# LSTM over image rows between two group norms: the convolved inputs kept as f32 and copied into the state banks by ScalarE

## The chip, the cores and the metric

The kernel runs on one core of a Trainium2 chip. The metric is the device time of one execution in microseconds (us). Three runs of the kernel before gave a median of 709.94 us, from 704.29 to 713.18 us.

## The reference

The input `x` is (32, 128, 32, 32) in f32: 32 images, 128 channels, 32 by 32 pixels. Two blocks follow, each `x = x + f(group_norm(x))` with 32 groups. `f` of the first block is a masked input convolution followed by an LSTM that steps over the 32 rows of the images; the state is 128 channels for 32 x 32 (image, column) positions:

```python
def step(carry, x_row):
    h, c = carry
    hc = conv(h, w_s2s) + b_s2s            # 1 x 3 over positions
    gates = (x_row + hc) @ w_ih.T + bias   # 4 x 128
    i, f, g, o = jnp.split(gates, 4, axis=-1)
    c = jax.nn.sigmoid(f) * c + jax.nn.sigmoid(i) * jnp.tanh(g)
    h = jax.nn.sigmoid(o) * jnp.tanh(c)
    return ((h, c), h)
```

`x_row` is the input convolution (1 x 3, its right tap masked to zero) of the normed images, one image row at a time. `f` of the second block is a 3 x 3 convolution whose weights are partly masked to their centre.

## The kernel before

Everything stays in on-chip memory, in `img` (128 channels x 32 images x 1024 pixels, four bytes a pixel). There are three stages, one after the other.

**Stage 1, the input convolution, one image at a time.** SyncE issues the loads (`load_x`), VectorE takes the statistics (`image_stats`) and the group norm's chain of small steps (`chain_mean`, `chain_var`, `chain_rstd`) for four images at once, seven images ahead of the convolution (`STATS_AHEAD`). ScalarE norms an image into `xn0` (`norm_image`). GpSimd or ScalarE, in turn, makes its f16 high part `hi0`, and GpSimd the rest `lo0`. TensorE's `input_conv` does twelve matmuls into two PSUM banks (`y_bank`). There are two slots of `xn0`, `hi0`, `lo0` and of pairs of banks. The result goes back to `img` as two f16 halves: ScalarE writes the high half (`high_xs`), VectorE the low one (`low_xs`). The weights are scaled, turned and split in between, at fixed places of each engine's program (`scale_weights` before image 7 is stored, `split_weights`, `last_weights`).

**Stage 2, the LSTM, in 96 items.** An item is one image row of one block of images: three blocks (`BLOCKS`) of 11, 10 and 11 images, so 352 or 320 columns. Every engine works through its own list of items in order, and semaphores tie them. TensorE's item `it` is:

- `close_conv(it)`: three matmuls, the right tap of the state convolution, which end the sum in the bank `zbank(it)` (there are two, used in turn);
- a wait for `z_lo_done`, and then `open_conv(it + 1)`: two matmuls with `spread` (a scaled identity) that bring the two f16 halves of the convolved input into the next bank, and six of the state convolution;
- a wait for `z_hi_done`, and twelve matmuls of the four gates of item `it`, the last two of the first pair after `z_lo`.

ScalarE's item `it` is the four gates of `it`, `high_z(it + 1)` (which reads `zbank(it + 1)` and writes `z_hi`), and `tc`, the tanh of the cell of `it`. VectorE forms the cell (L605, L609), `z_lo` of the next item (L590), the state and its two f16 halves (L614 to L619) and a transpose (L624). GpSimd multiplies the forget gate with the cell (L731) and adds the transposed state and the input into `img` (L739).

**Stage 3, the 3 x 3 convolution.** The change leaves it as it is but for the number that its chunks of statistics begin with.

Of the kernel before, what the change touches and what calls it, by code (L numbers as in the profile page):

```python
# [15 lines left out]
P = 128  # L16
# [12 lines left out]
XS_SCALE = 2.0 ** -14  # L29
# [10 lines left out]
CH = 4  # L40
CHUNKS = B // CH
GN_STEPS = 11
# [4 lines left out]
STATS_AHEAD = 7  # L47
# [24 lines left out]
def build_network(nc, x, w_i2s, b_i2s, w_s2s, b_s2s, w_ih, b_ih, b_hh, w_conv, b_conv, consts, out):  # L72
# [4 lines left out]
    with ExitStack() as ctx:  # L77
# [20 lines left out]
        bn = sb("bn", [P, CH, 2, 6], F32)  # L98
# [16 lines left out]
        with ExitStack() as s01:  # L115
# [13 lines left out]
            spread = sb("spread", [P, P], F16, s01)  # L129
            raw_cb = sb("raw_cb", [P, P], F32, s01)  # L130
            mask = sb("mask", [P, P], F32, s01)
            with ExitStack() as s0:
                xn0 = [sb(f"xn0{i}", [P, HW], F32, s0) for i in range(2)]
                hi0 = [sb(f"hi0{i}", [P, HW], F16, s0) for i in range(2)]
                lo0 = [sb(f"lo0{i}", [P, HW], F16, s0) for i in range(2)]
                raw_i = sb("raw_i", [P, P, 3], F32, s0)
                raw_s = sb("raw_s", [P, P, 3], F32, s0)
                raw_g = sb("raw_g", [P, GATES, P], F32, s0)
                raw_c = sb("raw_c", [P, P, 9], F32, s0)
                turn_i = sb("turn_i", [P, 2, P], F32, s0)  # L140
                turn_c = sb("turn_c", [P, 9, P], F32, s0)
            with ExitStack() as s1:
# [8 lines left out]
                hh = [sb(f"hh{i}", [P, B * W + 2], F16, s1) for i in range(2)]  # L151
                hl = [sb(f"hl{i}", [P, B * W + 2], F16, s1) for i in range(2)]
# [17 lines left out]
        spread_done = sem("spread_done")  # L170
# [23 lines left out]
        xs_hi_done = sem("xs_hi_done")  # L194
        xs_lo_done = sem("xs_lo_done")
# [40 lines left out]

        def padded(t, half, dh, dw):
# [20 lines left out]
        def xs_part(b, s, part):  # L258
            return img[:, b, H // 2 * s:H // 2 * (s + 1), part, :]
# [8 lines left out]

        def wgroup(n):
            return ps[:, 4 + n, 0:[2, 3, 4][n] * P].rearrange("p (a b) -> p a b", b=P)  # L270

        bias_T = ps[:, 4, 3 * P:4 * P]
        bias_ps = bias_T[96:97].rearrange("p (q n) -> p q n", q=Q)
        gate_bias_ps = ps[:, 5, 3 * P:3 * P + GATES]
# [3 lines left out]

        wconv_ps = ps[:, 4:7, 0:3 * P].rearrange("p d (e o) -> p d e o", o=P)
# [12 lines left out]
        def _(sp):  # L292
            def images(q, b, n):
                return img32[32 * q:32 * q + 32, b:b + n].rearrange("p b h w -> p b (h w)")

            def load_x(b):

                if b >= 2 * CH:

                    sp.wait_ge(x_in[b % (2 * CH)], QUARTERS_IN * (b // (2 * CH)))  # L300
                for q in QUARTERS:
                    sp.dma_start(images(q, b, 1), x_q[q, :, b:b + 1, :]).then_inc(x_in[b % (2 * CH)], 16)

            for b in range(STATS_AHEAD):
                load_x(b)
                if b == 0:
                    sp.dma_start(group_mean[:], consts[1]).then_inc(group_in, 16)
# [10 lines left out]
            for b in range(STATS_AHEAD, B):  # L318
                load_x(b)

            def place_blocks():

                sp.wait_ge(split_done, 4)
# [62 lines left out]
        def _(v):  # L386
# [23 lines left out]
            def bn_aggr(g):  # L410

                v.wait_ge(bn_done, 2 * CH * (g + 1))
                apart()
                for j in range(CH):
# [5 lines left out]
            def chain_mean(g):  # L420

                v.wait_ge(mean_ready, g + 1)
                v.tensor_tensor(dev[:], mv[:, :, 0], gn_ps[:, 0:CH], ALU.subtract).then_inc(gn_step, 1)
                v.tensor_tensor(dev_ps, mv[:, :, 0], gn_ps[:, 0:CH], ALU.subtract).then_inc(gn_step, 1)
                gn_wait(g, 2)
                v.tensor_tensor(dev2_ps, dev_ps, dev[:], ALU.mult).then_inc(gn_step, 1)
                gn_wait(g, 3)
                v.tensor_tensor(vdev[:], dev2_ps, mv[:, :, 1], ALU.add).then_inc(gn_step, 1)

            def chain_var(g):  # L430

                v.wait_ge(var_ready, g + 1)
                v.tensor_scalar(var_eps[:], gn_ps[:, CH:2 * CH], 1e-5, None, ALU.add).then_inc(gn_step, 1)

            def chain_rstd(g, i=0):

                v.wait_ge(sd_done, g + 1)
                v.reciprocal(rs0[:], sd[:]).then_inc(gn_step, 1)
                v.reciprocal(rs_ps, sd[:]).then_inc(gn_step, 1)
                gn_wait(g, 7)  # L440
                v.tensor_tensor(newton_ps, rs_ps, rs0[:], ALU.mult).then_inc(gn_step, 1)
                gn_wait(g, 8)
                v.scalar_tensor_tensor(out=rs_ps, in0=newton_ps, scalar=-0.5 / ACT_SCALE ** 2, in1=var_eps[:],
                                       op0=ALU.mult, op1=ALU.mult).then_inc(gn_step, 1)
                gn_wait(g, 9)
                v.scalar_tensor_tensor(out=rstd[i][:], in0=rs_ps, scalar=1.5, in1=rs0[:],
                                       op0=ALU.add, op1=ALU.mult).then_inc(gn_step, 1)
                gn_wait(g, 10)
                v.scalar_tensor_tensor(out=nbias[i][:], in0=gn_ps[:, 0:CH], scalar=-1.0, in1=rstd[i][:],
                                       op0=ALU.mult, op1=ALU.mult).then_inc(gn_step, 1)  # L450


            v.memset(hh[0][:], 0.0).then_inc(hh_done, NB - 1)
            v.memset(hh[1][:], 0.0).then_inc(hh_done, 1)
            v.memset(hl[0][:], 0.0).then_inc(hl_done, NB - 1)
            v.memset(hl[1][:], 0.0).then_inc(hl_done, 1)

            def image_stats(b):
                v.wait_ge(x_in[b % (2 * CH)], QUARTERS_IN * (b // (2 * CH) + 1))
                apart()  # L460
                bn_stats(image(b), b % CH)

            def scale_z_weights():
# [5 lines left out]
                step(v.tensor_reduce(top[:, 1:2], raw_s[:], AX.XY, ALU.max, apply_absolute_value=True))  # L469
                settle()  # L470
# [48 lines left out]
            def split_weights():  # L519

                split(1, ws_hi, ws_lo)
# [4 lines left out]
            def last_weights():  # L526

                v.wait_ge(prep_T, 4)
                v.memset(cell[:], 0.0).then_inc(c_done, NB)
                v.wait_ge(wall_hi_done, 1)  # L530
                v.tensor_tensor(gate_bias[:], gate_bias_ps, bsum[:, 1:1 + GATES], ALU.add).then_inc(gate_bias_done, 1)
                bias_weights()
                v.tensor_tensor(wall_lo[:], wconv_ps, wall_hi[:], ALU.subtract).then_inc(split_done, 1)
# [9 lines left out]
            def low_xs(b):  # L543

                for s in range(2):
                    v.wait_ge(xs_hi_done, 2 * b + s + 1)
                    v.scalar_tensor_tensor(out=xs_part(b, s, 1), in0=rows(y_bank(b, s)), scalar=XS_SCALE,
                                           in1=xs_part(b, s, 0), op0=ALU.mult, op1=ALU.subtract).then_inc(xs_lo_done, 1)

            image_stats(0)  # L550
            image_stats(1)
            scale_z_weights()
            image_stats(2)
            image_stats(3)
            bn_aggr(0)
            split(0, wi_hi, wi_lo)
            chain_mean(0)
            image_stats(4)
            chain_var(0)
            image_stats(5)  # L560
            chain_rstd(0)
            image_stats(6)
            for b in range(B):
                g, j = b // CH + 1, b % CH
                ahead = g < CHUNKS
                if ahead and j == 1:
                    chain_mean(g)
                if ahead and j == 2:
                    chain_var(g)
                if b + STATS_AHEAD < B:  # L570
                    image_stats(b + STATS_AHEAD)
                if ahead and j == 0:
# [590 lines left out]
```

## Time and profile before

| | us |
|---|---|
| median of the timed runs | 709.94 |
| the profiled execution, its own time | 712.78 |
| its span, first to last instruction | 711.0 |
| first matmul of the input convolution | 24.24 |
| first gate activation of stage 2 | 139.84 |
| stage 3 in its first tiled matmuls | 499.51 |

The profile comes from one execution. The span leaves out 1.8 us around the first and the last instruction. TensorE's matmuls are pipelined, so the duration of one (about 310 ns in stage 2) is longer than the step from one start to the next.

### The profile page before, as it was taken

How to read it: one execution, taken by the hardware profiler on the slowest of the kernel's cores; microseconds unless marked ns; L12 is line 12 of the kernel's file. 1: busy time of each engine (PE TensorE's matmuls, PEld its weight loads, DVE VectorE, ACT ScalarE, POOL GpSimd, SP SyncE). 2: the span in 40 equal slices, each digit the busy share in tenths (PEclk: the TensorE clock that was granted, in tenths of full speed). 3: DMA queues.
4: the chain of work that ended last, by engine and by line, in shares of the span. 5: the costliest groups of instructions: out<-in, count | busy, mean ns of one | idle time of the engine just before them, and what ended most of it. 6: DMA issues, size and time to landing. Idle time of an engine off the chain costs nothing.

```text
span 711.0 us, 15705 instructions
## 1 busy us (share of the span) xinstructions
PE 630.9 (89%) x5152; PEld 391.7 (55%) x5152; DVE 559.0 (79%) x1236; ACT 441.2 (62%) x779; POOL 426.0 (60%) x380
## 2 busy tenths in 40 slices
PE   1577889899999999999999999973899998988886
PEld 0233433378888888888888888851333333333332
DVE  5698998499999999999999999997576667666431
ACT  1595878777777777777777777774343444334310
POOL 0484687555555555555555555558676777577660
PEclk9998999999999999999999999995799999999997
DMA  9999900004441244442144443105799999999994
GB/s 224 238 265 274 151 5 8 1 0 60 59 60 31 28 59 59 59 59 37 22 59 59 59 59 44 15 1 129 192 283 254 284 267 251 262 254 269 274 258 126
DMA packets 96396, 90.61 MB, mean 127 GB/s; under 512 B 78240, under 2 KB 79520, under 8 KB 96288
## 3 DMA queue, kind: packets, MB, share of 16 engines
q1 hardware_dynamic: 89632, 71.09, 44.8%
q10 hardware_dynamic: 6720, 18.93, 10.0%
q8 instruction: 27, 0.44, 0.3%
q14 instruction: 17, 0.14, 0.1%
HBM read 35.07 MB, written 16.78 MB: 73 GB/s over the span
## 4 chain that ended last, share of the span: by engine, by line
PE 60%; SPq 21%; DVE 8%; DMA 3%; issue 3%; POOL 2%; ACT 2%; ACTq 0%; POOLq 0%; DVEq 0%
SPq L340 11%; PE ps L1009 7%; PE ps L1095 7%; SPq L346 6%; PE ps L1042 5%; PE ps L1046 4%; PE ps L1043 4%; PE ps L1056 4%; PE ps L1054 4%; PE ps L1055 4%; PE ps L1012 4%; PE ps L1000 4%; PE ps L959 3%; PE ps L960 2%; DMA shifted<-pad 2%
## 5 line engine op out<-in xcount | busy, mean ns | idle before, releaser
L731 POOL TENSOR_TENSOR fc<-gate,cell 128x352 f32<-128x352 f32 (+1 forms) x96 | 107.4, 1119 | 153.6 <-ACT gate L859 153.6
L766 POOL COPY shifted<-pad 32x1124 f32<-32x1124 f32 x128 | 142.9, 1116 | 58.6 <-DVE pad L646 52.4
L859 ACT ACTIVATE gate<-ps,gate_bias 128x352 f32<-128x352 f32 (+1 forms) x288 | 146.6, 548 | 47.6 <-PE ps L1046 31.8
L1095 PE MATMUL ps<-shifted,wt_hi 128*32 128x512 f16 x1536 | 110.7, 395 | 19.1 <-DMA shifted<-pad 19.1
L653 DVE SCALAR_TENSOR_TENSOR img<-ps,y_unscale,img 128x512 f32<-128x512 f32 x64 | 47.9, 748 | 82.9 <-PE ps L1095 82.8
L880 ACT ACTIVATE pad<-img,nbias,rstd 128x1024 f16<-128x1024 f32 x32 | 39.8, 1245 | 89.5 <-PE ps L1095 84.1
L739 POOL TENSOR_TENSOR img<-hT,xr 128x352 f32 (+3 forms) x96 | 87.0, 907 | 2.7 <-DVE hT L624 2.6
L408 DVE BATCH_NORM_STATS2 bn<-img 128x6 f32<-128x512 f32 x120 | 76.4, 680 | 10.7 <-DMA img<-in_x_dram 10.7
L721 POOL TENSOR_TENSOR lo<-xn,hi 128x1024 f16<-128x1024 f32 x32 | 68.1, 2131 | 19.0 <-PE ps L960 12.3
L1095 PEld LDWEIGHTS ps<-shifted,wt_hi 128*32 128x32 f16 x1536 | 35.5, 97 | 76.7 <-DMA shifted<-pad 24.0
L1042 PE MATMUL ps<-z_hi,wg_hi 128*128 128x352 f32 (+1 forms) x192 | 70.7, 371 | 2.3 <-ACT z_hi L848 2.2
L866 ACT ACTIVATE tc<-cell 128x352 f32<-128x352 f32 (+1 forms) x96 | 47.0, 490 | 27.3 <-DVE cell L609 27.3
L1056 PE MATMUL ps<-z_lo,wg_hi 128*128 128x352 f32 (+1 forms) x192 | 61.1, 318 | 0.0
L1054 PE MATMUL ps<-z_hi,wg_hi 128*128 128x352 f32 (+1 forms) x192 | 61.0, 318 | 0.0
L1055 PE MATMUL ps<-z_hi,wg_lo 128*128 128x352 f32 (+1 forms) x192 | 60.9, 317 | 0.0
L1043 PE MATMUL ps<-z_hi,wg_lo 128*128 128x352 f32 (+1 forms) x192 | 60.4, 318 | 0.0
L1085 PE MATMUL ps<-pad,wc_hi 128*128 128x512 f16 x128 | 52.0, 408 | 5.7 <-DVE pad L646 5.7
L614 DVE TENSOR_TENSOR hrow<-gate,tc 128x352 f32<-128x352 f32 (+1 forms) x96 | 49.4, 514 | 7.7 <-ACT tc L866 0.6
L605 DVE TENSOR_TENSOR ps<-ps,gate 128x352 f32<-128x352 f32 (+1 forms) x96 | 49.0, 511 | 7.9 <-ACT gate L859 7.7
L1095 PE MATMUL ps<-shifted,wt_lo 128*32 128x512 f16 x768 | 55.0, 393 | 0.0
L590 DVE SCALAR_TENSOR_TENSOR z_lo<-ps,z_unscale,z_hi 128x352 fp32r<-128x352 f32 (+1 forms) x96 | 54.1, 564 | 1.2 <-ACT z_hi L848 1.2
L848 ACT ACTIVATE z_hi<-ps,z_unscale 128x352 fp32r<-128x352 f32 (+1 forms) x96 | 54.0, 562 | 0.0
(138 smaller groups left out, 1435.5 us busy)
## 6 DMA issues: line engine op xcount, KB each, us to landing
shifted<-pad SPq DMA_DIRECT2D x128, 140.4 KB, 4.3
shifted<-pad ACTq DMA_DIRECT2D x128, 140.4 KB, 4.3
img<-in_x_dram SPq DMA_DIRECT2D x128, 128.0 KB, 3.4
xr<-in_x_dram SPq DMA_DIRECT2D x64, 256.0 KB, 5.6
out_dram<-img SPq DMA_DIRECT2D x60, 256.0 KB, 4.7
shifted<-shifted SPq DMA_DIRECT2D x2, 562.0 KB, 6.1
out_dram<-img SPq DMA_DIRECT2D x16, 64.0 KB, 1.7
raw_c<-in_L_conv_W_dram SPq DMA_DIRECT2D x4, 144.0 KB, 3.2
```

The lines of the kernel that those rows point to most:

```text
L340: sp.dma_start(shift_to(slot, e, q), shift_from(slot, e, q)).then_inc(shifted_in[slot], 16)
L408: v.bn_stats(bn[:, j, s, :], src[:, 512 * s:512 * s + 512]).then_inc(bn_done, 1)
L731: pool.tensor_tensor(fc[s % 2][:, 0:n], gate[s % 2][0][:, 0:n], cell[:, W * b0:W * b1], ALU.mult).then_inc(fc_done, 1)
L739: pool.tensor_tensor(img32[:, b0:b1, 2 * j + s // NB, :], hT[s % 2][:, 0:width(s % NB)].rearrange("p (b w) -> p b w", w=W), xr[:, slot, b0 ...
L766: pool.tensor_copy(flat(shifted[b % SLOTS][32:64, q]).bitcast(F32), flat(pad[b % SLOTS][32 * q:32 * q + 32]).bitcast(F32)).then_inc(unshif ...
L859: act.activation(gbank(s, m)[:, 0:n] if m == 1 else gate[p][m][:, 0:n], gbank(s, m)[:, 0:n], ACT.Tanh if gt == G_GATE else ACT.Sigmoid, bi ...
L1042: pe.matmul(gbank(s, m)[:, 0:n], wg_hi[:, GATE_ORDER[m], :], z_hi[:, 0:n], start=True, stop=False)
L1043: pe.matmul(gbank(s, m)[:, 0:n], wg_lo[:, GATE_ORDER[m], :], z_hi[:, 0:n], start=False, stop=False)
L1054: pe.matmul(gbank(s, m)[:, 0:n], wg_hi[:, GATE_ORDER[m], :], z_hi[:, 0:n], start=True, stop=False)
L1055: pe.matmul(gbank(s, m)[:, 0:n], wg_lo[:, GATE_ORDER[m], :], z_hi[:, 0:n], start=False, stop=False)
L1056: pe.matmul(gbank(s, m)[:, 0:n], wg_hi[:, GATE_ORDER[m], :], z_lo[:, 0:n], start=False, stop=True).then_inc(gate_ready, 1)
L1095: ins = pe.matmul(bank[32 * q:32 * q + 32], w[:, d, q, :], padded(shifted[b % SLOTS][:, q, part, :], s, d - 1, 0), start=False, stop=(m == ...
```

## The change

- `img` holds the convolved input as one f32 instead of two f16 halves. `high_xs` and `low_xs` are replaced by one copy of 1024 columns an image (`store_xs`), on ScalarE for even images and on VectorE for odd ones. `spread` is gone.
- In stage 2 `open_conv` loses its two matmuls with `spread`, and row 0 has no `open_conv` at all. ScalarE copies the f32 inputs from `img` into the z bank (`load_xs`), and the state matmuls add to what stands there. TensorE waits for `xs_loaded` ahead of `open_conv`, where it waited for `z_lo_done`.
- Stage 1 has three slots instead of two (`CONV_SLOTS`), statistics in chunks of 1, 2, 3, 4, ... images (`FIRST_COUNTS`) with an order of statistics written out by hand (`STATS_BY`, `CHAIN_AT`), stores that lag by two images, the f16 high part by ScalarE for three images of four, 18 images loaded ahead of the late weights, and image 0 loaded over two queues. The preparation of weights is cut up and moved, and the zeroing of the states goes from VectorE to GpSimd.

```diff
-            for b in range(STATS_AHEAD):
+            for q in QUARTERS[:2]:
+                load_quarter(sp, 0, q)
+            sp.dma_start(group_mean[:], consts[1]).then_inc(group_in, 16)
+            for b in range(1, LOADED_FIRST):
                 load_x(b)
...
+            def store_xs(b):
+
+                v.wait_ge(xconv_done, b + 1)
+                v.tensor_copy(image(b), flat(x_banks(b))).then_inc(xs_odd_done, 1)
...
+FIRST_COUNTS = (1, 2, 3, 4, 4, 4, 4, 4, 4, 2)
+CHAIN_AT = {0: 1, 1: 2, 4: 3, 7: 4, 11: 5, 15: 6, 19: 7, 23: 8, 27: 9}
+STATS_FIRST = 3
+STATS_BY = (6, 7, 8, 10, 11, 12, 14) + tuple(range(15, B + 1)) + (B,) * 7
+CONV_SLOTS = 3
+EVAC_LAG = 2
+SCALE_AT, TURN_CONV_AT = 13, 17
...
             def high_z(it, s):
 
                 n = width(s % NB)
                 act.wait_ge(z_ready, it + 1)
+                act.wait_ge(xs_loaded, it + 1)
                 act.activation(z_hi[:, 0:n], zbank(s)[:, 0:n], ACT.Identity, scale=z_unscale[:]).then_inc(z_hi_done, 1)
 
-            def item(j, s, last):
+            def load_xs(it, s, t):
+
+                n = width(s % NB)
+                b0, b1 = BLOCKS[s % NB]
+                act.wait_ge(z_lo_done, Z_AHEAD + it - 1)
+                act.activation(zbank(s)[:, 0:n].rearrange("p (b w) -> p b w", w=W), img32[:, b0:b1, t, :],
+                               ACT.Copy).then_inc(xs_loaded, 1)
+
+            def item(j, s, last, loads):
...
                 act.wait_ge(c_done, NB + it + 1)
                 act.activation(tc[p][:, 0:n], cell[:, W * b0:W * b1], ACT.Tanh).then_inc(tc_done, 1)
+                if loads:
+                    load_xs(it + 2, s + 2, 2 * j + (s + 2) // NB)
...
+            load_xs(0, 0, 0)
+            load_xs(1, 1, 0)
             high_z(0, 0)
...
-                for half in range(2):
-                    ins = pe.matmul(z.rearrange("p (b w) -> p b w", w=W), spread[:], img[:, b0:b1, t, half, :],
-                                    start=(half == 0), stop=row0 and half == 1)
...
-                if not last:
-
-                    pe.wait_ge(z_lo_done, it + 1)
-                    open_conv(2 * j + (s + 1) // NB, s + 1, (k + 1) % NB, zero_state and s + 1 < NB)
+                if not last and not (zero_state and s + 1 < NB):
+
+                    pe.wait_ge(xs_loaded, it + 2)
+                    open_conv(2 * j + (s + 1) // NB, s + 1, (k + 1) % NB)
 
                 pe.wait_ge(z_hi_done, it + 1)
```

## Rows read from the trace of the kernel before

**Rows 1.** Page, part 1: busy time, share of the span and instructions of each engine.

```profile
PE 630.9 (89%) x5152; PEld 391.7 (55%) x5152; DVE 559.0 (79%) x1236; ACT 441.2 (62%) x779; POOL 426.0 (60%) x380
```

**Rows 2.** Windows by stage: length, busy of the five engines, clock, DMA share, GB/s.

```profile
24.00:136.00 112.00, 94.69 (x434) 42.78 (x434) 92.51 (x244) 87.52 (x119) 83.10 (x48) 0.97 0.58 138
141.00:469.00 328.00, 326.96 (x2125) 263.46 (x2124) 305.37 (x650) 257.62 (x558) 184.24 (x185) 1.00 0.32 45
480.00:711.00 231.00, 196.85 (x2528) 76.05 (x2528) 134.11 (x277) 79.31 (x74) 150.71 (x133) 0.93 0.86 239
```

**Rows 3.** Groups by line, 200 to 440 us: count, busy us, mean ns, idle before.

```profile
L859 ACT ACTIVATE gate<-ps,gate_bias 128x352 f32<-128x352 f32 (+1 forms) x204 | 103.9, 549 | 33.1 <-PE ps L1046 21.7 <-DVE hrow L614 11.4
...
L848 ACT ACTIVATE z_hi<-ps,z_unscale 128x352 fp32r<-128x352 f32 (+1 forms) x68 | 38.3, 563 | 0.0
...
L866 ACT ACTIVATE tc<-cell 128x352 f32<-128x352 f32 (+1 forms) x68 | 33.3, 490 | 18.3 <-DVE cell L609 18.3
...
L1000 PE MATMUL ps<-img,spread 128*128 x136 | 30.7, 308 | 0.0
```

**Rows 4.** Timeline, one turn of stage 2: start us, length us, engine, line.

```profile
302.26 0.53 ACT L859 ACTIVATE gate<-ps,gate_bias 128x320 f32<-128x320 f32 x1 [0.43 <-PE ps L1046]
...
303.10 0.94 ACT L859 ACTIVATE gate<-ps,gate_bias 128x320 f32<-128x320 f32 x2
...
303.55 0.46 PE L1000 MATMUL ps<-img,spread 128*128 x2
...
303.85 0.46 PE L1009 MATMUL ps<-hh,ws_hi 128*128 128x352 f16 x2
303.92 0.57 ACT L848 ACTIVATE z_hi<-ps,z_unscale 128x352 fp32r<-128x352 f32 x1
...
304.21 0.49 DVE L609 TENSOR_TENSOR cell<-ps,fc 128x320 f32<-128x320 f32 x1
...
304.63 0.44 PE L1042 MATMUL ps<-z_hi,wg_hi 128*128 128x352 f32 x1
304.74 0.47 ACT L866 ACTIVATE tc<-cell 128x320 f32<-128x320 f32 x1 [0.24 <-DVE cell L609]
...
305.40 0.48 PE L1046 MATMUL ps<-z_lo,wg_hi 128*128 128x352 f32 x2
...
305.75 0.55 ACT L859 ACTIVATE gate<-ps,gate_bias 128x352 f32<-128x352 f32 x1 [0.55 <-DVE hrow L614]
```

**Rows 5.** Timeline, the first item of stage 2, ScalarE.

```profile
139.84 0.55 ACT L859 ACTIVATE gate<-ps,gate_bias 128x352 f32<-128x352 f32 x1 [1.17 <-PE ps L1046]
...
142.44 0.50 ACT L866 ACTIVATE tc<-cell 128x352 f32<-128x352 f32 x1 [0.29 <-DVE cell L609]
```

**Rows 6.** Timeline of stage 1: first images' statistics, first and last convolution matmuls.

```profile
7.92 1.29 DVE L408 BATCH_NORM_STATS2 bn<-img 128x6 f32<-128x512 f32 x2 [4.89 <-DMA img<-in_x_dram]
...
24.24 0.58 PE L959 MATMUL ps<-hi,wi_hi 128*128 128x512 f16 x1 [5.33 <-POOL hi L719]
...
135.43 0.38 PE L959 MATMUL ps<-lo,wi_hi 128*128 128x512 f16 x1
...
135.64 0.38 PE L960 MATMUL ps<-lo,wi_hi 128*128 128x496 f16 x1
```

**Rows 7.** Groups by line, 24 to 136 us.

```profile
L721 POOL TENSOR_TENSOR lo<-xn,hi 128x1024 f16<-128x1024 f32 x32 | 68.1, 2131 | 19.0 <-PE ps L960 12.3 <-ACT hi L808 5.4
L547 DVE SCALAR_TENSOR_TENSOR img<-ps,img 128x512 f16<-128x512 f32 x62 | 39.4, 676 | 6.8 <-ACT img L813 6.8
L801 ACT ACTIVATE xn<-img,nbias,rstd 128x1024 f32<-128x1024 f32 x31 | 38.4, 1239 | 2.9 <-POOL lo L721 1.8
L813 ACT ACTIVATE img<-ps 128x512 f16<-128x512 f32 x63 | 33.8, 585 | 11.9 <-PE ps L960 11.8
```

**Rows 8.** Windows around TensorE's longest halt in stage 1 (columns as in rows 2).

```profile
48.00:52.00 4.00, 2.73 (x12) 1.05 (x12) 3.88 (x10) 3.89 (x7) 3.92 (x3) 1.00 0.94 242
52.00:56.00 4.00, 0.00 (x0) 0.00 (x0) 3.76 (x13) 1.98 (x2) 2.86 (x2) 0.83 0.94 261
56.00:60.00 4.00, 3.19 (x8) 1.16 (x9) 3.85 (x11) 0.00 (x0) 0.00 (x0) 0.50 0.94 265
```

More of the change, by code:

```diff
@@ L1 @@
+import itertools
 import struct
@@ L256, in y_bank, with x_banks, xs_stored @@
             return ps[:, 2 * (b % 2) + s, :]
-        def xs_part(b, s, part):
-            return img[:, b, H // 2 * s:H // 2 * (s + 1), part, :]
+        def x_banks(b):
+            first = 2 * ((b + 1) % CONV_SLOTS)
+            return ps[:, first:first + 2, :]
+        def xs_stored(engine, b):
+            return engine.wait_ge(xs_odd_done if b % 2 else xs_even_done, b // 2 + 1)
         def rows(t):
@@ L551, in _ @@
+            image_stats(0)
+            bn_aggr(0)
+            chain_mean(0)
+            top_z_weights()
+            chain_var(0)
+            scale_z_weights()
+            chain_rstd(0)
             image_stats(1)
-            scale_z_weights()
+            split(0, wi_hi, wi_lo)
             image_stats(2)
[L554 to L560, printed above, removed]
@@ L561, in _ @@
-            chain_rstd(0)
-            image_stats(6)
+            bn_aggr(1)
             for b in range(B):
-                g, j = b // CH + 1, b % CH
-                ahead = g < CHUNKS
-                if ahead and j == 1:
+                g = CHAIN_AT.get(b)
+                if b >= EVAC_LAG and b % 2:
+                    store_xs(b - EVAC_LAG)
+                if g is not None:
                     chain_mean(g)
-                if ahead and j == 2:
+                for i in range(STATS_BY[b - 1] if b else STATS_FIRST, STATS_BY[b]):
+                    image_stats(i)
+                if g is not None:
@@ L952, in input_conv @@
[L952 to L967 removed]
+                pe.wait_ge(split_done, 3 + d)
@@ new lines, in turn_conv @@
+                for e in range(3):
+                    ins = pe.transpose(wconv_ps[:, e, :], turn_c[:, 3 * d + e, :], ident[:])
+                if d == 0:
+                    pe.wait_ge(bias_ready, 1)
+                    pe.wait_ge(wgt_done, 1)
+                    for k in range(GATES):
+                        ins = pe.matmul(gate_bias_ps[:, k:k + 1], wgT[:, k, :], bsum[:, 0:1], start=True, stop=True)
+                if d == 2:
+                    pe.wait_ge(bias_ready, 2)
+                    ins = pe.transpose(bias_T, bias_col[:], ident[:])
@@ new lines, in turn_conv, with taps, input_high @@
+                ins.then_inc(prep_T, 1)
+            def taps(b, s, w, t, first, last):
+                bank = rows(x_banks(b)[:, s, :])
+                pixels = rows(t[:])[:, H // 2 * s:H // 2 * (s + 1)]
+                pe.matmul(bank, w[:, 1, :], pixels, start=first, stop=False)
+                return pe.matmul(bank[:, :, 1:W], w[:, 0, :], pixels[:, :, 0:W - 1], start=False, stop=last)
+            def input_high(b, s):
+                pe.wait_ge(hi0_done, b + 1)
+                if b >= CONV_SLOTS:
+                    xs_stored(pe, b - CONV_SLOTS)
+                taps(b, s, wi_hi, hi0[b % CONV_SLOTS], True, False)
+                taps(b, s, wi_lo, hi0[b % CONV_SLOTS], False, False)
```

341 lines of the change are left out of this document (175 added, 166 removed).

## The prediction

> **What bounds the kernel now.** I read the page's busy shares first: TensorE is busy for 89% of the span, the next engine for 79% [rows 1]. That is a mean over three stages, so the windows by stage come second [rows 2]. In stage 1 TensorE works 94.7 of 112 us and no engine is full: the stage lives on waits between engines. In stage 2 TensorE works 327 of 328 us. In stage 3 it works 197 of 231 us with the DMA engines at 0.86; the change doesn't touch it, and I carry it over at its length. Third come the groups by line inside stage 2, and fourth the timeline of one turn, because what the change puts into stage 2 is a copy in the middle of ScalarE's list and a wait in the middle of TensorE's.
>
> The period of stage 2 is 240 us over 68 items, 3.53 us [rows 3]. TensorE issues without a gap, 23 matmuls an item about 0.15 us apart. ScalarE has 18.3 us of idle before `tc` and 33.1 us before the gates in the 68 items, 0.76 us an item. A copy of a block fits into that as work. Whether it fits in time is the question.
>
> **Stage 2: what goes.** The two `spread` matmuls start 0.30 us ahead of the six that follow [rows 4]. If nothing else changed, TensorE's item would be 0.30 us shorter.
>
> **Stage 2: what comes, and where.** `load_xs` is one ScalarE instruction of 352 or 320 columns, f32, from on-chip memory to PSUM. The trace has no such copy. Its nearest rows are `tc` (memory to memory, 490 ns) and `z_hi` (out of PSUM, 563 ns) [rows 3]. I take 0.50 us, with ends of 0.41 (the step from one ScalarE start to the next, below) and 0.60.
>
> The wait is the larger thing. TensorE's item `it` is close(it), wait, open(it + 1), gates(it). The wait is now for `xs_loaded` of `it + 2`, that is for the copy of item `it + 1`. ScalarE makes that copy at the end of its item `it - 1`, behind the tanh `tc(it - 1)`. In the timeline, call the item whose gates start at 302.26 item A (320 columns) and the next one B. TensorE closes B, and opens the item after B from 303.55; ScalarE has `tc(A)` at 304.74 [rows 4]. The copy that the opening needs can start only after that, at about 305.15, and end at 305.65. So `open` moves from 303.85 (its first state matmul) to 305.75 or so, and queued behind it on TensorE are the twelve gate matmuls of B, which before waited only for `z_hi(B)` and started at 304.63. ScalarE's next gate waits for them, and `tc(B)` waits for that gate. This closes a ring that the kernel before doesn't have: gates on ScalarE, tanh, copy, open, gates on TensorE, gates on ScalarE.
>
> The ring, leg by leg:
> - first gate to `tc` on ScalarE: 304.74 - 302.26 = 2.48 us at 320 columns [rows 4], 142.44 - 139.84 = 2.60 at 352 [rows 5]; mean over two wide blocks and one narrow, 2.56. Nothing in it gets shorter: `tc` follows the end of the cell sum (304.21 + 0.49), which hangs on the third gate.
> - `tc` start to the end of the copy: 0.41 (two gates start at 303.10, then `z_hi` at 303.92) + 0.50 = 0.91.
> - hand-over from ScalarE to TensorE: `z_hi` ends at 304.49, the matmul behind it is entered at 304.63, so 0.12 to 0.14. I take 0.12.
> - six matmuls of `open`: 6 x 0.15 = 0.90 wide, less narrow; 0.88.
> - four gate matmuls before L1046: the last of `open` is through at 303.85 + 0.90 = 304.75, L1046 starts at 305.40: 0.65.
> - L1046 to the first gate on ScalarE: 305.75 - 305.40 = 0.35, rather more where the wait is exposed; 0.38.
>
> Sum 2.56 + 0.91 + 0.12 + 0.88 + 0.65 + 0.38 = 5.50 us for an item against 3.53, so 1.97 more. The wait is there from TensorE's item 2 to item 94, 93 times: 93 x 1.97 = +183 us. With the ends of each leg (copy 0.41 to 0.60, hand-over 0.05 to 0.20, the others within 0.05) the period is 5.30 to 5.75, and the term +165 to +206. The 0.30 us of the removed matmuls is in the 0.88 already. VectorE is busy 305 of 328 us now [rows 2], but with 5.5 us an item it has two thirds of its time used and bounds nothing; the same holds for GpSimd.
>
> The Trainium skill (ScalarE: Activation LUTs, Step-by-step: what each stage is for) gives 0.833 ns an element whatever the function. For 352 columns that would be 0.29 us; the trace has 0.49 for `tc`, so the rate alone is not the duration here. With 0.29 the ring would be 5.29 us.
>
> **Stage 1: start.** Image 0 has its statistics at 7.92 us [rows 6]. Chunk 1 holds only image 0, so its convolution can start near 16 us instead of 24.24. But the norm of image 1 stands behind `chain_rstd(1)`, and VectorE takes the statistics of images 3, 4 and 5 in front of that. At some 260 GB/s [rows 8] an image of 512 KB takes 2.0 us, image 5 is in at about 18.5, its statistics end at 19.8, the chain at 20.8, the norm (1.24 [rows 7]) at 22.0 and the high part near 23. So the even stream of convolutions starts with image 1 at 23 us. Before, image 0 started it at 24.24.
>
> **Stage 1: rate.** Before: 32 images from 24.24 to 135.86, 3.49 each. Work for one image after: TensorE 12 x 0.215 = 2.6 (the step from 135.43 to 135.64 [rows 6]); GpSimd 2.13 + a quarter of a cast of 1.04; ScalarE 1.24 + 3/4 of 1.05 + half of a copy that now takes 2 x 0.585 [rows 7], 2.6; VectorE loses 2 x 0.676 and gains half of a copy of about 1.2, which leaves some 2.7 with the statistics and the chains. The floor is TensorE's 2.6. Three slots cover more of the halts; the worst now is `scale_weights` on VectorE, during which TensorE had nothing from 51 to 56 us [rows 8]. It stays, at image 13, with one slot more of cover. I take 2.9 an image: 31 x 2.9 + 23 = 113 against 135.86, so -23. At 2.7 it is -29, at 3.3 -11.
>
> **Between the stages.** Before, the first gate came 4.0 us after the last convolution matmul (135.86 to 139.84 [rows 5, 6]), over the stores, an opening and `z_hi`. After, `z_hi(0)` needs no opening, but VectorE's `z_lo(0)` stands behind its store of image 31: 1.1 + 0.6 + 0.5, some 2.2. That gives -2.
>
> **Sum.** The profiled execution's own time was 712.8; 712.8 + 183 - 25 = 871. It lay 2.8 us above the median of the timed runs, so against that the forecast is 868 us.
>
> **Rivals.**
> - *The copy is not on the path, and the kernel gets faster.* That is so if the copy ends before TensorE has closed the next item. Then TensorE's item is up to 0.30 us shorter; ScalarE's `z_hi` ends at 304.49, only 0.26 ahead of the 304.75 at which TensorE is ready for it, so 0.12 to 0.30 an item: 712.8 - 25 - 96 x 0.2 = 669, or 666 against the median. For it: ScalarE has 0.76 us idle an item. Against it: the point from which it decides is that the copy would have to end 2 us earlier than ScalarE's order has it. I give it 0.04.
> - *The ring and, on top, TensorE's clock falls.* At half clock (1.2 GHz) the twelve matmuls and the opening cost double. The trace shows the clock full with 2.73 busy of 4 us, and fallen only after some 6 us without any matmul [rows 8]. In the ring TensorE would work about 3.2 of 5.5 us, with a halt of 2.3. The legs on TensorE are 0.88 + 0.65 + 0.38 = 1.9 us; at the half level in half of the items, 93 x 0.5 x 1.9 gives +88, with the later close behind it up to +125: about 970. I give it 0.06.
> - The Trainium skill (TensorE: Matmul & The Clock Gate, A second HAM failure mode: psum-queue depth-cycling) tells of a kernel whose clock swung because of short idle stretches between groups of matmuls. It would speak for this rival; rows 8 don't show it.
> - *Partial ring.* Some copies come early enough and the time stays within 2%: this needs a period near 3.8. Nothing in the order allows it; 0.02.
>
> **How the numbers follow.** The ring as summed has 0.88. Its own range: +165 and -29 gives 846 after the correction of 2.8, +206 and -11 gives 905. I let the low end reach a little further for a copy that overlaps the tanh more than assumed: 840 to 905. What lies outside is the faster rival, the clock rival and the far corners. Chances: faster by over 2% 0.04, within 2% 0.02 (about what a measurement of this kernel can tell from no change), slower 0.94.
>
> **What the profile after would show.** Stage 2 about 520 us long, TensorE busy for under two thirds of it, and its idle time in front of L1009's successor put down to the copy on ScalarE. The copy itself at 0.45 to 0.55 us. ScalarE idle before its first gate for 1.5 to 2 us an item, clock at 1.00. Stage 1's last convolution matmul at 105 to 120 us. The prediction is wrong if TensorE issues stage 2 without gaps, if the idle time sits before the gates with `z_hi` as its releaser, or if the clock falls there.

## The result, and the profile after

The changed kernel takes 895.73 us (median of 4 runs, 894.41 to 898.1), the kernel before 709.61 beside it (4 runs). The ratio is 1.263, with a 95% interval of 1.257 to 1.269: slower. The profiled execution had an own time of 895.51 us and a span of 893.6.

The page of the changed kernel, parts 1, 2 and 4; it answers to [rows 1].

```profile
span 893.6 us, 15496 instructions
...
PE 661.7 (74%) x4968; PEld 408.1 (46%) x4968; DVE 545.1 (61%) x1207; ACT 471.0 (53%) x838; POOL 398.6 (45%) x377
...
PEclk9997999999989988998999899899885999999999
...
PE 41%; SPq 20%; ACT 13%; DVE 11%; issue 11%; DMA 3%; ACTq 1%; DVEq 0%
```

No engine is near full any more, and TensorE's busy time has grown by 31 us though the trace has 184 matmuls fewer. Work cannot explain 183 us more of span; waits must. The third line has a second reading: the granted clock is no longer full through the middle of the span.

The windows by stage of the changed kernel (columns as in [rows 2]).

```profile
24.00:132.00 108.00, 96.23 (x453) 47.25 (x453) 81.52 (x217) 86.99 (x98) 74.89 (x45) 0.94 0.64 141
132.00:640.00 508.00, 344.58 (x1881) 267.96 (x1881) 300.15 (x632) 285.10 (x629) 159.84 (x180) 0.91 0.21 29
...
662.00:893.00 231.00, 197.83 (x2540) 77.16 (x2538) 137.80 (x285) 81.79 (x79) 152.46 (x135) 0.94 0.84 239
```

The timeline of ScalarE's gates at both ends of stage 2 gives the split between the stages.

```profile
127.60 0.56 ACT L908 ACTIVATE gate<-ps,gate_bias 128x352 f32<-128x352 f32 x1 [2.62 <-PE ps L1115]
128.05 0.52 ACT L908 ACTIVATE ps<-ps,gate_bias 128x352 f32<-128x352 f32 x1
...
662.80 0.56 ACT L908 ACTIVATE gate<-ps,gate_bias 128x352 f32<-128x352 f32 x1 [0.87 <-PE ps L1115]
```

- Stage 1: the first gate comes at 127.60 instead of 139.84 [rows 5], so 12.2 us earlier.
- Stage 2: from the gates of item 0 to those of item 95 it is 662.80 - 127.60 = 535.2 us, 5.63 an item. Before it was 476.01 - 139.84 = 336.2, 3.54 an item. That is 199.0 more.
- Stage 3: from there to the end of the span 893.6 - 662.8 = 230.8, before 711.0 - 476.0 = 235.0. The change doesn't touch it; 4.2 less.

The sum is -12.2 + 199.0 - 4.2 = +182.6, and the spans differ by 182.6.

Groups by line, 200 to 600 us, of the changed kernel. They answer to [rows 3].

```profile
L908 ACT ACTIVATE gate<-ps,gate_bias 128x352 f32<-128x352 f32 (+1 forms) x211 | 109.8, 548 | 156.3 <-PE ps L1115 147.2 <-PE ps L1128 7.0
...
L915 ACT ACTIVATE tc<-cell 128x352 f32<-128x352 f32 (+1 forms) x71 | 34.4, 485 | 13.7 <-DVE cell L629 13.7
L1070 PE MATMUL ps<-hh,ws_hi 128*128 128x352 f16 (+1 forms) x142 | 33.4, 318 | 128.7 <-ACT ps L896 128.7
...
L896 ACT ACTIVATE ps<-img 128x352 f32 (+1 forms) x71 | 31.4, 443 | 0.0
```

L1070 is the first state matmul of `open`. TensorE waits in front of it for the copy at L896, 1.81 us on average over the 71 items. ScalarE then waits 2.1 us for L1115, the gate matmuls queued behind `open`. Two idle times, each released by the other engine: that is what a closed ring looks like in this view.

The timeline of one turn at full clock, changed kernel, beside [rows 4].

```profile
306.05 0.56 ACT L908 ACTIVATE gate<-ps,gate_bias 128x352 f32<-128x352 f32 x1 [2.05 <-PE ps L1115]
...
307.81 0.57 ACT L889 ACTIVATE z_hi<-ps,z_unscale 128x352 fp32r<-128x352 f32 x1
...
308.65 0.50 ACT L915 ACTIVATE tc<-cell 128x352 f32<-128x352 f32 x1 [0.27 <-DVE cell L629]
309.05 0.42 ACT L896 ACTIVATE ps<-img 128x320 f32 x1
...
309.53 0.45 PE L1070 MATMUL ps<-hh,ws_hi 128*128 128x320 f16 x2 [1.94 <-ACT ps L896]
...
311.00 0.48 PE L1115 MATMUL ps<-z_lo,wg_hi 128*128 128x352 f32 x2
...
311.36 0.55 ACT L908 ACTIVATE gate<-ps,gate_bias 128x352 f32<-128x352 f32 x1 [1.89 <-PE ps L1115]
```

The ring takes 311.36 - 306.05 = 5.31 us here. The turn before it took 5.96 (its first gate is at 300.09): there the matmuls of L1126 to L1128 start 0.27 apart instead of 0.16, so part of that turn ran at the lower level of the clock. The mean of the stage, 5.63 at a granted clock of 0.91, lies between the two.

Stage 1 in the timeline of TensorE, and the windows around its longest halt, both of the changed kernel. They answer to [rows 6] and [rows 8].

```profile
25.89 0.59 PE L1015 MATMUL ps<-hi,wi_hi 128*128 128x512 f16 x1 [1.66 <-ACT hi L840]
...
74.16 0.37 PE L984 MATMUL ps<-mv,group_mean 128*128 128x4 f32 x1 [6.84 <-DVE mv L439]
...
124.95 0.38 PE L1016 MATMUL ps<-lo,wi_hi 128*128 128x496 f16 x1
```

```profile
68.00:72.00 4.00, 0.00 (x0) 0.00 (x0) 3.64 (x8) 1.50 (x2) 2.90 (x2) 0.79 0.94 253
72.00:76.00 4.00, 1.84 (x6) 1.01 (x7) 3.69 (x13) 0.00 (x0) 0.00 (x0) 0.50 1.00 268
76.00:80.00 4.00, 4.00 (x13) 1.76 (x12) 3.21 (x11) 2.92 (x3) 1.60 (x1) 0.50 1.28 203
```

The even stream starts at 25.89, the last convolution matmul at 124.95: 3.20 us an image, where 2.9 from 23 on was forecast. The halt of 6.84 us is still there with the third slot, and behind it the clock stays at 0.50 until 80 us.

### The profile page after: what moved, and what is told of

Its sections match the earlier page's. It is cut to its first block, busy times and chain, and to the rows that moved or that the text cites. A ratio compares the mean times of both kernels' runs of the same rounds, so it can differ in the third digit from the quotient of the medians.

```text
span 893.6 us, 15496 instructions
## 1 busy us (share of the span) xinstructions
PE 661.7 (74%) x4968; PEld 408.1 (46%) x4968; DVE 545.1 (61%) x1207; ACT 471.0 (53%) x838; POOL 398.6 (45%) x377
## 4 chain that ended last, share of the span: by engine, by line
PE 41%; SPq 20%; ACT 13%; DVE 11%; issue 11%; DMA 3%; ACTq 1%; DVEq 0%
PE ps L1070 8%; SPq L364 8%; SPq L253 6%; PE ps L1163 5%; ACT gate L908 5%; SPq L370 5%; ACT ps L896 4%; DVE ps L625 4%; DVE cell L629 4%; PE ps L1112 4%; PE ps L1111 4%; PE ps L1074 3%; PE ps L1115 3%; DMA shifted<-pad 3%; PE ps L1015 3%
## 5 line engine op out<-in xcount | busy, mean ns | idle before, releaser
L908 ACT ACTIVATE gate<-ps,gate_bias 128x352 f32<-128x352 f32 (+1 forms) x288 | 149.6, 548 | 212.8 <-PE ps L1115 201.1
L758 POOL TENSOR_TENSOR fc<-gate,cell 128x352 f32<-128x352 f32 (+1 forms) x96 | 87.8, 915 | 370.8 <-ACT gate L908 370.8
L1070 PE MATMUL ps<-hh,ws_hi 128*128 128x352 f16 (+1 forms) x186 | 44.1, 320 | 169.3 <-ACT ps L896 169.3
L1070 PEld LDWEIGHTS ps<-hh,ws_hi 128*128 128x128 f16 x186 | 10.6, 97 | 204.9 <-ACT ps L896 144.8
L1111 PE MATMUL ps<-z_hi,wg_hi 128*128 128x352 f32 (+1 forms) x192 | 77.0, 403 | 1.9 <-ACT z_hi L889 1.9
L1126 PE MATMUL ps<-z_hi,wg_hi 128*128 128x352 f32 (+1 forms) x192 | 69.7, 363 | 0.0
L1127 PE MATMUL ps<-z_hi,wg_lo 128*128 128x352 f32 (+1 forms) x192 | 69.6, 363 | 0.0
L1128 PE MATMUL ps<-z_lo,wg_hi 128*128 128x352 f32 (+1 forms) x192 | 69.5, 362 | 0.0
L1112 PE MATMUL ps<-z_hi,wg_lo 128*128 128x352 f32 (+1 forms) x192 | 67.7, 355 | 0.0
```

The costliest lines, as they stand in the source:

```text
L758: pool.tensor_tensor(fc[s % 2][:, 0:n], gate[s % 2][0][:, 0:n], cell[:, W * b0:W * b1], ALU.mult).then_inc(fc_done, 1)
L908: act.activation(gbank(s, m)[:, 0:n] if m == 1 else gate[p][m][:, 0:n], gbank(s, m)[:, 0:n], ACT.Tanh if gt == G_GATE else ACT.Sigmoid, bi ...
L1070: pe.matmul(z, w[:, tap, :], before[0][:, W * b0 + tap:W * b1 + tap], start=False, stop=False, skip_group_check=True)
L1111: pe.matmul(gbank(s, m)[:, 0:n], wg_hi[:, GATE_ORDER[m], :], z_hi[:, 0:n], start=True, stop=False)
L1112: pe.matmul(gbank(s, m)[:, 0:n], wg_lo[:, GATE_ORDER[m], :], z_hi[:, 0:n], start=False, stop=False)
L1126: pe.matmul(gbank(s, m)[:, 0:n], wg_hi[:, GATE_ORDER[m], :], z_hi[:, 0:n], start=True, stop=False)
```

## The experiments

Two questions were open. Is the 199 us of stage 2 the place of the copy in ScalarE's list, or the amount of work, or the clock? And what holds stage 1, so that three slots bring so little? Most kernels below change one thing in the changed kernel; the ones on stage 1 start from its version with the copy moved.

**The copy at the head of the item (e1).**

```diff
+                if loads:
+                    load_xs(it + 2, s + 2, 2 * j + (s + 2) // NB)
                 act.wait_ge(h_done, it + 1)
 ...
                 act.activation(tc[p][:, 0:n], cell[:, W * b0:W * b1], ACT.Tanh).then_inc(tc_done, 1)
-                if loads:
-                    load_xs(it + 2, s + 2, 2 * j + (s + 2) // NB)
```

> The changed kernel, with one edit: ScalarE copies the convolved input for item it + 2 at the head of its item it, ahead of the four gates, instead of behind the tanh. Nothing else moves, and the number of instructions is the same. Theory (ring): the copy is done before TensorE has closed item it + 1, the ring gates, tanh, copy, opening, gates is open again, and what binds is ScalarE's gates and z_hi followed by four gate matmuls, some 3.45 to 3.55 us an item against 5.63. Total 895.7 - 95 x 2.1 = 695 us, range 680 to 710, TensorE's clock back at 1.00. Rival (the cost is ScalarE's extra work, or sums that start from a copied bank, wherever the copy stands): the period stays above 5 us and the total above 830 us.

It took 694.12 us (4 runs), 0.978 of the kernel before timed beside it (0.973 to 0.983). A period of 3.54 us, the same instructions as in the changed kernel, and 201.6 us less. The groups by line of this kernel, 200 to 440 us:

```profile
L910 ACT ACTIVATE gate<-ps,gate_bias 128x352 f32<-128x352 f32 (+1 forms) x204 | 103.0, 544 | 0.0
...
L917 ACT ACTIVATE tc<-cell 128x352 f32<-128x352 f32 (+1 forms) x68 | 33.3, 490 | 18.0 <-DVE cell L629 18.0
L896 ACT ACTIVATE ps<-img 128x352 f32 (+1 forms) x69 | 31.7, 460 | 6.4
...
L1111 PEld LDWEIGHTS ps<-z_hi,wg_hi 128*128 128x128 f32 x136 | 25.4, 187 | 27.1 <-issue 27.1
```

The idle 33.1 us that ScalarE had before its gates [rows 3] is gone: the copy (31.7 us) all but fills it. No wait for the copy is left. TensorE's weight loads are idle 0.40 us an item in front of L1111, the matmul that reads `z_hi`; in the kernel before it was 7.5 / 68 = 0.11 (the line stands with the last experiment). The period, 3.54 us, is that of the kernel before. So as work the copy costs nothing that can be seen, and its place, with the clock that came with it, cost the 199 us. That the copies are too much for ScalarE is out.

**Two places between (e2, e3).** The copy between the fourth gate and `z_hi`, and the copy between `z_hi` and the tanh; the line is moved as above.

> The changed kernel with the copy between the fourth gate and z_hi on ScalarE. Ring theory: the opening starts when the copy ends, 1.66 (four gates) + 0.44 + 0.1 = 2.2 us after the first gate, then 0.88 + 0.65 + 0.38: a period of 4.1 to 4.3 us and a total of 895.7 - 95 x 1.45 = 760 us (745 to 775). Rival (amount of work on ScalarE): within 15 us of the run with the copy first.

> The changed kernel with the copy between z_hi and the tanh on ScalarE. Ring theory: copy from 2.2 to 2.65 us after the first gate, hand-over 0.1, then 0.88 + 0.65 + 0.38: a period of 4.65 to 4.75 us at full clock, total 895.7 - 95 x 0.93 = 807 us (790 to 825, the upper part if the clock falls at times as it does in the changed kernel). Rival (amount of work on ScalarE): the same time as the two other places of the copy.

They took 755.4 us and 797.63 us (one run each), with periods of 4.13 and 4.56; the first period lies in its forecast range and the second 0.1 us below it, and both totals lie in theirs. The waits of each, 200 to 440 us, engine and line, its releaser, then the sum, the count and the longest; first the copy after the gates:

```profile
ACT gate L908 <- PE ps L1115: 63.1, 58, 1.2
PE ps L1070 <- ACT ps L896: 45.5, 58, 0.8
```

And with the copy before the tanh:

```profile
ACT gate L908 <- PE ps L1115: 79.5, 52, 1.7
PE ps L1070 <- ACT ps L896: 64.7, 53, 1.3
```

TensorE's wait for the copy is 0.78 us an item in the one, 1.22 in the other and 1.81 in the changed kernel. The four places give 3.54, 4.13, 4.56 and 5.63 us: each step that the copy goes back in the list lengthens the ring. The two between had the clock at 1.00 through stage 2, so in the last figure alone a part is the clock's.

**Is the clock part of it (e4)?** The changed kernel, with nine more matmuls an item on TensorE while it waits for the copy. They write into a gate bank that the real gate matmuls overwrite, so they add nothing to the output.

```diff
+            def fill(t, s, k):
 ...
+                for _ in range(FILL):
+                    pe.matmul(gbank(s - 1, 0)[:, 0:width(k)], ws_hi[:, 0, :], before[:, W * b0:W * b1],
+                              start=True, stop=True)
 ...
+                    if not zero_state:
+                        fill(2 * j + (s + 1) // NB, s + 1, (k + 1) % NB)
                     pe.wait_ge(xs_loaded, it + 2)
```

> The changed kernel with nine extra f16 matmuls an item on TensorE (9 x 0.15 = 1.35 us) in the stretch in which it waits for the copy; they write into the gate bank that the next gate matmul starts afresh, so no result changes. Theory (the clock is worth what the ring sum lacks): the granted clock in stage 2, 0.91 now, goes to 1.00, and the period falls from 5.63 to the 5.31 us that two neighbouring gates at full clock show: total 895.7 - 95 x 0.32 = 865 us (858 to 875), although TensorE does 130 us more of work. Rival (the low clock is not on the path, or the ring is longer for another reason): the total stays at 895 or rises.

It took 861.84 us (one run), 33.9 less than the changed kernel, with some 800 matmuls more. The windows of this kernel, 140 to 460 us, and the wait that is left between 200 and 440:

```profile
140.00:460.00 320.00, 279.47 (x1789) 209.03 (x1789) 200.40 (x423) 187.80 (x420) 106.86 (x120) 0.99 0.24 33
```

```profile
PE ps L1071 <- ACT ps L897: 28.8, 45, 0.7
```

The clock is back at 0.99 and the period is 5.30 us, the length of the full-clock turn in the changed kernel (5.31). TensorE still waits for the copy, 28.8 / 45 = 0.64 us an item, so the added matmuls are through before it comes. So of the 2.10 us an item that the change costs, 1.76 are the ring itself and 0.34 the clock: 95 x 0.34 = 32 us, and the total says 34.

**Stage 1: the third slot (e6).** The copy at the head, and `CONV_SLOTS = 2` instead of 3; the first copies then wait for the last two stored images instead of the two before them.

> The kernel with the copy first, with two slots of normed images and banks in stage 1 instead of three; the two first copies of stage 2 wait for the last two images. Theory A (the third slot is what makes stage 1 shorter): the first gate comes at 135 to 142 us instead of 127.6, total 702 to 708. Theory B (the cheaper stores and the earlier start give the gain; the slot covers only small halts): the first gate at 128 to 133 us, total 694 to 701.

It took 705.33 us (one run), and its first gate came at 129.15 us, as theory B had it. With three slots two executions of the kernel with the copy at the head had it at 125.98 and 126.93. By that the third slot is worth some 3 us. The total is 11 us higher, above theory B's range: but from the gates of item 95 to the end of the span this execution took 237.4 us, those two 232.4 and 225.9. That is stage 3, which these edits leave alone; over the executions of all the kernels here it ran from 225.9 to 237.4. So totals of a few runs cannot place a gain of 3 us, and stage 1 is read by its first gate; that gate has a spread too, 125.98 to 127.60 in the six executions with the changed kernel's stage 1.

**Stage 1: the work on scales moved back (e5).** The copy at the head, `scale_weights` from image 13 to 24, the turning of the convolution weights to 26, the turned rows to 27, 28 and 29.

```diff
-TURN_STATE, TURN_GATES, TURN_ROWS = 6, 16, (20, 24, 28)
+TURN_STATE, TURN_GATES, TURN_ROWS = 6, 16, (27, 28, 29)
 ...
-SCALE_AT, TURN_CONV_AT = 13, 17
+SCALE_AT, TURN_CONV_AT = 24, 26
```

> The kernel with the copy first (694 us), with the scaling of the second convolution's weights moved from image 13 to image 24 on VectorE, and their turning from images 17 to 28 to images 26 to 29. Theory (the miss of stage 1): VectorE's 8.8 us for the scaling stand ahead of the statistics that TensorE's group matmul of image 15 waits for; TensorE stood still for 6.8 us there and then ran at half clock for about 5 us. At image 24 nearly all statistics are done, so the halt and the low clock go: the first gate, at 127.6 us in the changed kernel, comes at 117 to 121 us and the total is 694 - 8 = 686 us (682 to 690). Rival (the three engines are so full that the work only moves): first gate within 2 us of 127, total 692 to 698.

It took 700.46 us (4 runs; 0.984 of before, 0.971 to 0.998), with its first gate at 130.60: later, not earlier. The theory missed, and the rival (within 2 us of 127) too. The halts of TensorE in this kernel's timeline:

```profile
99.89 0.38 PE L1015 MATMUL ps<-hi,wi_hi 128*128 128x512 f16 x1 [2.75 <-DVE img L570]
...
110.05 0.45 PE L1001 MATMUL ps<-ident,turn_c 128*128 128x128 f32 x1 [2.74 <-DVE wall_lo L557]
...
118.21 0.41 PE L1001 MATMUL ps<-ident,turn_c 128*128 128x128 f32 x2 [2.25 <-DVE wall_lo L557]
```

The halt of 6.84 us is gone and 2.75 stands in its place. But each turning (L1001) now waits for VectorE's split of the turning before it, since they follow each other image by image, and the granted clock from 110 to 116 us is 0.52. One long halt had been traded for three shorter ones.

**Stage 1: an earlier start (e7).** The kernel just described, with the variance and `rstd` of the chain at image 0 (the one that the norm of image 1 waits for) taken ahead of the statistics of images 3 to 5.

```diff
+                if b == 0:
+                    chain_var(g)
+                    chain_rstd(g, g % 2)
                 for i in range(STATS_BY[b - 1] if b else STATS_FIRST, STATS_BY[b]):
                     image_stats(i)
-                if g is not None:
+                if g is not None and b > 0:
```

> The kernel with the late scaling, and the chain of the second chunk (images 1 and 2) on VectorE ahead of the statistics of images 3, 4 and 5 instead of behind them. Theory (start): image 1 is normed at about 19.5 us instead of 23.5, its convolution starts at 22 instead of 25.9, and of these 3.9 us two to three stay: 686 - 2.5 = 683 us. Rival: the third chunk's statistics are late by as much and TensorE waits there instead, total within 1 us of the late scaling alone.

It took 694.82 us (4 runs; 0.975, 0.962 to 0.989), the first gate at 128.63 against 130.60: the 2 us of the theory, on a base that had missed by more.

**The early chain alone, and the copy alone once more (e9, e8).** The early chain with `scale_weights` left at image 13, beside the kernel with the copy at the head, on one chip.

> The kernel with the copy first and, in stage 1, the chain of the second chunk ahead of the statistics of images 3 to 5; the scaling at its place of the changed kernel (image 13). Theory (start): 2 us less than the copy first, as between the late scaling with and without the early chain (first gate at 128.6 against 130.6 us): ratio 0.975, first gate at 124 us. Rival (TensorE's halt at image 15 takes it back): first gate at 126 us, the same ratio as the copy first.

> The kernel with the copy first once more, beside the two below on one chip: ratio to the kernel before 0.978, as in its first run (0.973 to 0.983).

695.71 us (6 runs; 0.979, 0.974 to 0.983) and 694.1 us (6 runs; 0.977, 0.973 to 0.982). The first gates are at 125.38 and 126.93, and both still have the long halt, 6.86 and 6.84 us. The early chain's first gate lies between its theory's 124 and the rival's 126. What the early start gains is below what these runs can tell.

**Both, and the turnings spaced (e10).** The early chain, `SCALE_AT, TURN_CONV_AT = 20, 22` and `TURN_ROWS = (23, 26, 29)`, on the same chip.

> The kernel above, with the scaling at image 20, and the three turnings of the late weights at images 23, 26 and 29, three apart, so that none waits for the split of the one before (in the late scaling they stood at 27, 28 and 29, and TensorE halted for 2.7 and 2.3 us in front of the second and the third). Theory (spacing): the halts of 2.3 to 2.8 us are gone, and the one of 6.8 us at image 15 with them; the first gate comes at 118 to 121 us, ratio 0.967 to 0.971. Rival (the halt follows the scaling, since VectorE has little spare time at image 20 too): a halt of 3 us or more in front of a group matmul at image 23, first gate at 123 to 126 us, ratio 0.973 to 0.978.

It took 689.94 us (6 runs), 0.971 of the kernel before (0.966 to 0.976). Its median is the lowest of all versions, below both kernels. The first gate is at 122.22, later than the forecast 118 to 121. The windows of this kernel over the images in which the turnings now lie:

```profile
64.00:84.00 20.00, 19.83 (x99) 9.63 (x98) 17.65 (x52) 17.47 (x19) 17.13 (x10) 1.00 1.03 229
84.00:104.00 20.00, 16.74 (x85) 7.94 (x83) 15.92 (x48) 16.13 (x16) 12.25 (x7) 1.00 0.35 44
104.00:124.00 20.00, 18.10 (x90) 9.38 (x88) 8.13 (x21) 16.60 (x25) 13.61 (x12) 1.00 0.03 4
```

None of the three is below full clock, where the changed kernel has 0.74 from 64 to 84 us. Behind the start of the even stream one halt over 2 us is left, 2.75 at 90.03. So the place of `scale_weights` did hold stage 1, for about 3 us: the kernel that differs only in these places (the early chain alone) had its first gate at 125.38, one execution each. Moved without spacing the turnings it gained nothing.

**What the removed matmuls were worth (e11).** The kernel before with the two `spread` matmuls left out from row 1 on and nothing in their place; the first state matmul starts the bank instead, and the convolved input is missing from rows 1 to 31.

```diff
-                for half in range(2):
-                    ins = pe.matmul(z.rearrange("p (b w) -> p b w", w=W), spread[:], img[:, b0:b1, t, half, :],
-                                    start=(half == 0), stop=row0 and half == 1)
                 if row0:
+                    for half in range(2):
+                        ins = pe.matmul(z.rearrange("p (b w) -> p b w", w=W), spread[:], img[:, b0:b1, t, half, :],
+                                        start=(half == 0), stop=half == 1)
```

> The kernel before, with the two spread matmuls of every opening from row 1 on left out and nothing in their place: the convolved input is missing in the state banks of rows 1 to 31. It asks what these matmuls were worth. Theory (several rings of nearly one length): the loop from ScalarE's first gate over z_hi and four gate matmuls back is 2.33 + 0.13 + 0.65 + 0.38 = 3.49 us, against a period of 3.54, and VectorE is busy 93% of the time; so the period falls by 0.05 to 0.12 us only, total -5 to -11 us, ratio 0.985 to 0.993. Rival (TensorE alone bounds stage 2, as its busy time of 99.7% says): the period falls by the whole 0.30 us, total -28 us, ratio 0.960.

It took 707.34 us (12 runs) against 710.06 (17), a ratio of 0.998 (0.994 to 1.001): no difference that can be told, so neither the theory (0.985 to 0.993) nor the rival (0.960). The windows of this kernel as in [rows 2], and its groups of 200 to 440 us:

```profile
141.00:469.00 328.00, 322.84 (x1946) 244.97 (x1946) 304.88 (x648) 258.31 (x558) 185.55 (x185) 1.00 0.32 45
```

```profile
L859 ACT ACTIVATE gate<-ps,gate_bias 128x352 f32<-128x352 f32 (+1 forms) x204 | 103.9, 549 | 32.4 <-PE ps L1047 27.7 <-DVE hrow L614 4.7
...
L1043 PEld LDWEIGHTS ps<-z_hi,wg_hi 128*128 128x128 f32 x138 | 25.8, 187 | 26.9 <-issue 26.9
```

L1043 here is L1042 of the kernel before, where the same groups have:

```profile
L1042 PEld LDWEIGHTS ps<-z_hi,wg_hi 128*128 128x128 f32 x136 | 25.4, 187 | 7.5 <-issue 3.7
```

Two of 23 matmuls are gone from an engine that was busy for 99.7% of the stage [rows 2], and the period is 3.53 us, 3.54 before. The 0.30 us come back as idle weight loads in front of the matmul that reads `z_hi`: 26.9 / 69 = 0.39 us an item for 7.5 / 68 = 0.11. ScalarE waits as long before its gates as in the kernel before (32.4 and 33.1 us). So beside TensorE ran a ring of nearly the same length, and in this kernel's timeline it closes: first gate at 299.81, `z_hi` from 301.57 to 302.12, L1043 at 302.25, L1047 at 302.94, next first gate at 303.35, which is 3.54 us. Which leg of it would have to be shortened was not tried. The busy 99.7% also hides small gaps: a matmul's 0.31 us cover two steps of 0.15.

## Why the prediction was right, and where it was off

The forecast was 868 us in a range of 840 to 905, and it came to 895.7. The miss of 27.7 us is made of four terms. That the time still lies in the range is in part luck: the range had no fall of the clock in it, and a ring summed 18 us too long hid more than half of that fall.

**The ring** was the right mechanism. The releaser was the one named, and moving one line removes all of it. Its legs at full clock, forecast and then measured:
- first gate to `tc`: 2.56, 2.60;
- `tc` to the end of the copy: 0.91, 0.82. The copy took 0.42 in this turn and 0.44 on average, where `tc` had stood in for it at 0.50;
- hand-over to TensorE: 0.12, 0.06;
- `open` and four gate matmuls: 0.88 + 0.65 = 1.53, 1.47;
- last gate matmuls to the first gate: 0.38, 0.36.

The sum is 5.31 instead of 5.50; over 93 items that is 18 us too many. (The copy and the opening of this turn are of 320 columns; the mean over all turns at full clock, from the kernel with the added matmuls, is 5.30.) The Trainium skill (ScalarE: Activation LUTs, Step-by-step: what each stage is for) gives a rate an element by which the prediction estimated 0.29 us for the copy; the runs have 0.42 to 0.48, so the rate alone is not the duration of so short a copy, and the neighbouring row was nearer.

**The clock** is the step that failed. The prediction wrote "clock at 1.00" for stage 2 and put its fall at 0.06. The granted clock was 0.91, and that is worth 32 to 34 us: the rival's mechanism, at a third of the +88 that it was priced at. By the prediction's last sentence a fall of the clock there was a sign of its being wrong. The rows it was judged by [rows 8] had one long halt in them and no row of short halts, and the argument took their silence for a no. They were misread too: TensorE's last matmul before that halt is at 50.35 (0.38 long), and 0.83 in the stretch from 52 to 56 says that the clock fell inside it, some 4 us into the halt and not after 6. With the ring 18 us below its forecast, the clock 32 above, and 95 turns instead of 93 (4 us), stage 2 came out 199 us longer where 183 were forecast, +16; rounding takes the rest. The Trainium skill (TensorE: Matmul & The Clock Gate, A second HAM failure mode: psum-queue depth-cycling) tells of a clock that swings by short idle stretches between groups of matmuls. This trace agrees: with waits of 1.8 us in turns of 5.6 some turns ran at the lower level in part and others at the full one, with a mean of 0.91.

**Stage 1** was overrated. Forecast was a first gate 25 us earlier, measured 12.2: +13. Of the 12.4 us between the forecast 115.2 and 127.6, 2.9 are the start (25.89 for 23), 0.3 the step between the stages (2.5 for 2.2, a good term), and 9 the rate, 3.20 for 2.9 us an image. (The ends of the range leave out the 2 us between the stages that the sum has; with them they are 844 and 903.) The sentence that failed is that `scale_weights` stays "with one slot more of cover". Here VectorE in the changed kernel, from where the halt begins:

```profile
65.86 1.95 DVE L520 TENSOR_TENSOR bsum<-brow 128x1 f32<-128x1 f32 x1
...
67.91 0.88 DVE L523 TENSOR_TENSOR top<-top 128x1 f32<-128x1 f32 x1
...
68.89 2.10 DVE L526 SCALAR_TENSOR_TENSOR top<-bias_top,top 128x1 f32<-128x1 f32 x1
```

VectorE is held from 63.47 to 72.25 us, and the small matmul at 74.16 waits for a chain of statistics behind it. A slot covers convolutions ready ahead; it doesn't bring forward an `rstd` that is queued behind the scales. That, with the half clock behind it, is worth the 3 us that moving and spacing it gave back. The other 7 us to the forecast 115.2 (from 122.22) no run took apart.

Half of those 8.8 us look like a wait of VectorE for GpSimd. GpSimd in the same stretch:

```profile
65.66 2.13 POOL L742 TENSOR_TENSOR lo<-xn,hi 128x1024 f16<-128x1024 f32 x1 [0.99 <-ACT hi L840]
67.73 1.05 POOL L740 CAST hi<-xn 128x1024 f16<-128x1024 f32 x1
68.86 2.12 POOL L742 TENSOR_TENSOR lo<-xn,hi 128x1024 f16<-128x1024 f32 x1
```

Each of VectorE's three long operations, on one element a partition, begins while one of these runs and ends with it: at 67.81, 68.79 and 70.99 where GpSimd's end at 67.79, 68.78 and 70.98. With `scale_weights` at image 24 GpSimd is free from 97.06 to 104.09 us; there the first of the three took 1.14 us, to 97.08, and the other two 0.16 each, and the whole of `scale_weights` 5.1 us instead of 8.8. So a part of what moving it gained may be that it met GpSimd less; that was not tried by itself.

**Stage 3 and the median.** Stage 3 was 4.2 us shorter in this execution, which nothing in the change explains; two executions of the kernel with the copy at the head differ by 6.5 us in it (232.4 and 225.9). And the profiled execution lay 0.2 below its median instead of 2.8 above it, +3. Together 16 + 13 - 4 + 3 = 28.

Of the signs that the prediction named, TensorE's wait for the copy, ScalarE's before its first gate (2.1 us for up to 2) and the length of stage 2 (535 for 520) came nearly as said; the last convolution matmul, 125 us for 105 to 120, and the clock did not. The prediction also gave the faster rival 0.12 to 0.30 us an item for the removed matmuls. The run without them puts that term at 0.04 us an item or less (the low end of its ratio, over 93 items); with the copy at the head the gain over before is stage 1's alone, 13 to 14 us by the first gate.

## What to carry to other kernels

- Before an instruction is added to an engine's list, write down who waits for it and what that waiter has queued behind it. A copy that fits an engine's idle time as work cost 199 us in one place and nothing that can be seen in another.
- A busy share of 99.7% is not proof of a bound: look for a ring of the same length before counting on matmuls saved.
- Where a change makes TensorE wait in every turn, price the clock too. And work that blocks an engine once is moved only as far as its followers keep their distance.
- When a tiny operation takes 1 to 2 us, lay the other engines' timelines beside it and compare the ends.

## What the runs showed of the chip

- The granted clock fell to a mean of 0.91 with waits of 1.8 us in turns of 5.6 us, and stayed at 1.00 with 1.22 us in 4.56 and at 0.99 with 0.64 us in 5.30. Nine more matmuls an item made the kernel 34 us faster.
- Operations of VectorE on one element a partition took 1.95, 0.88 and 2.10 us when an operation of GpSimd was running as they began, and 0.16 for two of them when none was. In all 13 profiled executions the long ones (0.82 to 2.11 us) end within 0.02 us of the end of such an operation. The traffic of the loads is not the cause: with `scale_weights` at image 24 the first still took 1.14 us, with the DMA share from 95 to 98 us at 0.00. The slow ones all read two tensors in memory; whether that decides it was not tried.
- The copy of 352 or 320 columns from memory to PSUM took 0.42 to 0.48 us.
